# A transformer stack with a routed expert layer on one core: the router's placement compared in halves and summed inside a context layer, context layer 5 behind the expert tiles, and the third norm's second root ahead of the copies

## The chip, the cores and the metric

The kernel runs on one core of a Trainium2 chip. The metric is the device time of one execution in microseconds. The kernel before was executed three times for its time and once more under the profiler.

## What is computed

Eight blocks of 100 tokens with 256 features, `x`, pass through four residual steps, each behind a layer norm (mean and variance of a token, epsilon 1e-5). What matters of the reference:

```python
x = x + jnp.tanh(g_xattn[0]) * _L0_xattn_ref(_layernorm(x), ctx_768, ...)   # attention over 361 context rows
x = x + jnp.tanh(g_ffn[0]) * _L0_ffn_ref(_layernorm(x), w_router, w1, b1, w2, b2)
x = x + jnp.tanh(g_xattn[1]) * _L1_xattn_ref(_layernorm(x), ctx_768, ...)   # ternary weights, int8 activations
x = x + jnp.tanh(g_ffn[1]) * _L1_ffn_ref(_layernorm(x), ...)                # 16 heads chosen by a gate

# _L0_ffn_ref
sel = jnp.argmax(softmax(x @ w_router), axis=-1)      # one of 8 experts for each token
for e in range(8):
    y = relu(x @ w1[e] + b1[e]) @ w2[e] + b2[e]
    out = out + ((sel == e) * wgt)[:, None] * y

# _L1_xattn_ref, for each of two attention layers Wa, and a linear layer before
qx = clip(round(x / i_scale), -128, 127);  i_scale = max(abs(x)) / 127
kv = bitnet_linear(image_embeds, Wa, ba)
```

## The kernel before, in words

The program is written by hand: each engine has a list of instructions in program order, and semaphores (`S[...]`) are the only link between the lists. Nothing is scheduled by a tool. TensorE is PE, VectorE is DVE, ScalarE is ACT, GpSimd is POOL, and SyncE (SP) issues most loads. T is 800 tokens, a half is 400 tokens or blocks 0 to 3 and 4 to 7. The stages, in order of time: the first attention; its residual and the second norm; the router; the expert tiles; the third norm; the second attention; its feed-forward part; the fourth norm; the gated heads.

**The router's placement.** Tokens are sorted by expert into tiles of 128 slots. DVE finds, for each token, its tile (`at_tile`, L859 and L861) and its slot in the tile as a row of 128 zeros and ones (`at_slot`, one compare of 100x1024 elements at L863, which increments `placed`). PE sums `at_slot` times `at_tile` over the eight blocks into bank 3 (L1709, eight matmuls of 28 columns, two instructions each). DVE makes of it `token_of`, the token in each slot (L866, L868), and increments `inverse_done`. POOL then gathers the rows of the first tiles from `x_slots` in DRAM with indirect DMAs (L483).

**Context layers.** The keys and values of the second attention don't hang on `x`. PE computes them as filler, as `last_context_layer(b)` for eight blocks b: four matmuls for keys (L1499) and six for values (L1507), in the rotating banks 4 to 7. ACT evicts each layer with two ACTIVATEs (L1313) and three copies (L1318), and increments `kv_out` five times. Layer 0 stands behind the router's scores, layers 1 to 3 between the rank matmuls and the sum L1709, layers 4 and 5 behind that sum, and 6 and 7 behind the expert tiles.

**Expert tiles.** PE waits for the evictions of six layers (`kv_out` at 30), `inverse_done` and the first gather (`xs_in0`), turns that tile (L1720, in bank 6, one of the rotating ones) and enters the loop over 14 tiles: 16 matmuls of two instructions for the hidden part (L1736), the turn of the next tile, and 8 such for the result (L1749). DVE adds the bias (L894), POOL scatters to `y_slots` (L489). SP loads each expert's weights into two buffers, released by PE's counts.

**The third norm.** SP loads `y_slots` back in four pairs of blocks. DVE adds them to `x` (L908), takes statistics of each block (L533, one block behind), gathers them for each half (L551) and writes the variance (L557, `ln_var`). ACT takes the root (L1176, `ln_std`). DVE makes its reciprocal (L563) and the shift (L564, `ln_shift`). ACT normalises blocks 0 to 3, 6 and 7 (L1179), DVE blocks 4 and 5 (L568). PE turns each half in two steps (L1451), and ACT copies each step to `xT` (L1183). On ACT one function, `layernorm_by_halves`, does root, normalisation and two copies of half 0, and then the same of half 1. DVE then takes the maxima of `xT` (L932), and through POOL's reduction over partitions the scale; it quantises `xT` (L602, L603), and PE's matmuls of the text projection start (L1457). The second norm uses the same functions with k = 2.

Of the kernel before, what the change touches and what calls it, by code (L numbers as in the profile page):

```python
# [6 lines left out]
ALU = mybir.AluOpType  # L7
ACT = mybir.ActivationFunctionType
# [11 lines left out]
HT = T // 2  # L20
# [17 lines left out]
         [(1, j) for j in range(0, 6)], [(1, j) for j in range(6, 12)], [(1, j) for j in range(12, 16)]]  # L38
OWN = (0, 3, 6)
NP = 4  # L40
NW = 3
# [88 lines left out]
def flamingo(nc, d):  # L130

    ctx = ExitStack()
    with ctx:
# [389 lines left out]
        def _(dve):  # L523
# [35 lines left out]
            def half_shift(k, h):  # L559

                bs = slice(4 * h, 4 * h + 4)
                dve.wait_ge(S["ln_std"], 2 * (k - 1) + h)
                link(dve.reciprocal(rstd[:, bs], std[:, bs]))  # L563
                dve.scalar_tensor_tensor(var[:, bs], mv[:, bs, 0], -1.0, rstd[:, bs], ALU.mult, ALU.mult)\  # L564
                    .then_inc(S["ln_shift"], 1)
                if h == 1:
                    for b in (4, 5):
                        dve.tensor_scalar(xn[:, b, :], x[:, b, :], mv[:, b, 0:1], rstd[:, b:b + 1],  # L568
                                          ALU.subtract, ALU.mult).then_inc(S["ln_out"], 1)
# [256 lines left out]
            for z in range(3):  # L826
                ins = dve.tensor_tensor(lead[:, z + 1, 4:12, :], lead[:, z, 4:12, :],
                                        lead[:, z, 4 - 2 ** z:12 - 2 ** z, :], ALU.add)
                if z < 2:
# [32 lines left out]
                              const("token", N)[:, :, None].to_broadcast([N, B, TILES]), ALU.mult)  # L862
            dve.tensor_tensor(at_slot, along_b(const("slot", N), SLOTS),  # L863
                              r_s[:, :, None].to_broadcast([N, B, SLOTS]), ALU.is_equal).then_inc(S["placed"], 1)
            dve.wait_ge(S["inverse_mm"], 1)
# [39 lines left out]
            for b in range(B + 1):  # L905
                if b < B:
                    dve.wait_ge(S[f"gathered{b // 2}"], 16)
                    dve.scalar_tensor_tensor(x[:, b, :], y_tok[:, b, :], top_w[:, b:b + 1], x[:, b, :],  # L908
                                             ALU.mult, ALU.add).then_inc(S["x2_done"], 1)
                if b >= 1:  # L910
                    dve.wait_ge(S["x2_done"], b)
                    ins = token_stats(b - 1)
                if b == 4:
                    link(ins)
                    link(gather_stats(0, 4))
                    half_variance(0)
                if b == 5:
                    half_shift(3, 0)
                if b == 7:
                    link(ins)  # L920
                    gather_stats(4, 7)
# [236 lines left out]
        def _(act):  # L1158
# [11 lines left out]

            def layernorm_by_halves(k):

                for h in range(2):
                    bs = slice(4 * h, 4 * h + 4)
                    act.wait_ge(S["ln_var"], 2 * (k - 1) + h)
                    act.activation(std[:, bs], var[:, bs], ACT.Sqrt).then_inc(S["ln_std"], 1)  # L1176
                    act.wait_ge(S["ln_shift"], 2 * (k - 2) + h + 1)
                    for b in range(4) if h == 0 else (6, 7):
                        act.activation(xn[:, b, :], x[:, b, :], ACT.Identity, bias=var[:, b:b + 1],  # L1179
                                       scale=rstd[:, b:b + 1]).then_inc(S["ln_act"], 1)  # L1180
                    for kk in range(2):
                        act.wait_ge(S["ln_turned"], 4 * (k - 1) + 2 * h + kk + 1)
                        act.copy(xT[:, kk, h * HT:(h + 1) * HT], psum[4 + 2 * kk + h][:, 0:HT])\  # L1183
                            .then_inc(S["xT_ready"], 1)

# [108 lines left out]
            for n in range(8):  # L1294
# [3 lines left out]
                               bias=cols[:, 4 + m:5 + m]).then_inc(S["h0_out"], 1)  # L1298
            layernorm_by_halves(2)
            act.wait_ge(S["logit_a"], 1)  # L1300
# [19 lines left out]

            for b in range(6):
                last_context_out(b)
# [9 lines left out]

            last_context_out(6)
            last_context_out(7)
            layernorm_by_halves(3)
            act.wait_ge(S["quantised"], 4)
# [92 lines left out]
        def _(pe):  # L1429
# [12 lines left out]
            def turn_tokens_half(k, h):  # L1442

                for kk in range(2):
                    for g in range(4):
                        b = 4 * h + g
                        if b in (4, 5):
                            pe.wait_ge(S["ln_out"], B + 2 * (k - 2) + b - 3)
                        else:
                            pe.wait_ge(S["ln_act"], 6 * (k - 2) + (b if b < 4 else b - 2) + 1)  # L1450
                        ins = pe.transpose(psum[4 + 2 * kk + h][:, g * N:(g + 1) * N], xn[:, b, kk * P:(kk + 1) * P],  # L1451
                                           ident[0:N, 0:N])
                    ins.then_inc(S["ln_turned"], 1)
# [31 lines left out]
            for n in range(4):  # L1485
                m, half = n // 2, n % 2
                layer(psum[4 + n][:, 0:HT], lambda k: w_q[:, k, m * P:(m + 1) * P],
                      lambda k: xT[:, k, half * HT:(half + 1) * HT], 2, 2).then_inc(S["q_mm"], 1)
            def last_context_layer(b):

# [3 lines left out]
                for m in range(2):  # L1494
                    j = 5 * b + m
                    if j >= 4:
                        pe.wait_ge(S["kv_out"], j - 3)
                    for k in range(2):
                        ins = pe.matmul(psum[4 + j % 4][:, 0:M], wa[m][:, k, :], qc[:, k, b, :],  # L1499
                                        start=k == 0, stop=k == 1)  # L1500
                    ins.then_inc(S["kv_mm"], 1)
                for c, (c0, rows_c) in enumerate(CH):
                    j = 5 * b + 2 + c
                    if j >= 4:
                        pe.wait_ge(S["kv_out"], j - 3)
                    for k in range(2):
                        ins = pe.matmul(psum[4 + j % 4][0:rows_c, 0:D], qc[:, k, b, c0:c0 + rows_c],  # L1507
                                        wkv[:, k], start=k == 0, stop=k == 1)
                    ins.then_inc(S["kv_mm"], 1)

            def ternary(name, n):
# [192 lines left out]
            pe.matmul(psum[1][0:N, 0:B * E0], ones, before, start=False, stop=True).then_inc(S["rank_mm"], 1)  # L1704
            for b in range(1, 4):
                last_context_layer(b)
            pe.wait_ge(S["placed"], 1)
            for b in range(B):
                ins = pe.matmul(psum[3][0:SLOTS, 0:2 * TILES], at_slot[:, b, :],  # L1709
                                at_tile[:, b].rearrange("p z t -> p (z t)"), start=b == 0, stop=b == B - 1)  # L1710
            ins.then_inc(S["inverse_mm"], 1)
            last_context_layer(4)
            last_context_layer(5)
            pe.wait_ge(S["kv_out"], 5 * 6)
            pe.wait_ge(S["inverse_done"], 1)
# [38 lines left out]

            last_context_layer(6)
            last_context_layer(7)
            pe.wait_ge(S["kv_out"], 5 * B)
# [72 lines left out]
            def turn_half(h):  # L1830

                for kk in range(2):
                    for g in range(4):
                        b = 4 * h + g
                        pe.wait_ge(S["ln_out"], B + 4 + b + 1)
                        ins = pe.transpose(psum[(4 if h == 0 else 6) + kk][:, g * N:(g + 1) * N],
# [182 lines left out]
```

## Time and profile before

| | us |
|---|---|
| time, median of 3 executions | 660.27 |
| lowest and highest of them | 658.64 and 660.91 |
| the profiled execution's own time | 658.99 |
| its span, first to last instruction | 657.2 |
| PE busy | 596.5 (91%) |
| DVE busy | 327.0 (50%) |
| ACT busy | 217.8 (33%) |
| POOL busy | 71.0 (11%) |
| chain that ended last | PE 83%, DVE 8%, ACT 4%, DMA 2% |

The mean granted clock of PE was 0.938 of full speed. The span is what the profiler saw between the first and last instruction; the time holds what lies around it, here 1.8 us. An engine's busy time is a sum over stages of quite different limits. The chain of waits follows the work back from the last instruction, at each step to what released it. The timeline gives instructions in order of time, neighbours of one kind merged; its bracket says how long the engine was idle before and which work ended that.

### The profile page before, as it was taken

Reading aid. Unit: us, or ns where it says so; the run is one execution under the profiler, and the core shown is the slowest. Engines: PE = TensorE matmul, PEld = TensorE weight load, DVE = VectorE, ACT = ScalarE, POOL = GpSimd, SP = SyncE. Lnnn points to the kernel's source line nnn. Section 1 sums busy time; section 2 is a strip of 40 time slices with the busy share of each in tenths; the row PEclk is TensorE's granted clock in tenths of the full one; section 3 lists DMA queues with packets and bytes.
Section 4 is the critical chain, followed back from the end, with each engine's and each line's share of the span. In section 5 each row is a group of like instructions: output and inputs, shape, how many; then the busy total and the mean of one; then the engine's idle time right before and its main releaser. Section 6 shows DMA issues by size and latency. Waiting matters only on the chain.

```text
span 657.2 us, 9281 instructions
## 1 busy us (share of the span) xinstructions
PE 596.5 (91%) x3603; PEld 393.2 (60%) x3603; DVE 327.0 (50%) x772; ACT 217.8 (33%) x508; POOL 71.0 (11%) x69
## 2 busy tenths in 40 slices
PE   6989999999979899999995489776699999999997
PEld 4755344444555778999994267445365555555653
DVE  3686766588746551212223567689624223221543
ACT  2543665656633363122114454381110000000100
POOL 0052000000017002232221000000100100000000
PEclk9999999999989969999998589687699999999999
DMA  8900000000016235999982000600443553330000
GB/s 204 331 13 17 1 1 1 2 2 2 2 33 205 71 126 185 335 332 347 341 308 67 0 0 6 220 0 1 135 138 96 188 206 96 97 96 1 0 26 25
DMA packets 25194, 69.93 MB, mean 106 GB/s; under 512 B 5142, under 2 KB 12918, under 8 KB 21318
## 3 DMA queue, kind: packets, MB, share of 16 engines
q1 hardware_dynamic: 21798, 58.16, 26.9%
q0 software_dynamic: 3360, 11.28, 4.9%
q8 instruction: 24, 0.39, 0.2%
q14 instruction: 12, 0.10, 0.0%
HBM read 64.62 MB, written 4.80 MB: 106 GB/s over the span
## 4 chain that ended last, share of the span: by engine, by line
PE 83%; DVE 8%; ACT 4%; DMA 2%; issue 1%; POOL 1%; SPq 0%; DVEq 0%; ACTq 0%; POOLq 0%
PE bank L1869 20%; PE bank L1457 12%; PE bank L1736 8%; PE bank L1749 7%; PE bank L1588 7%; PE bank L1905 7%; PE bank L1562 5%; PE bank L1606 3%; PE bank L1797 2%; PE bank L1531 2%; PE bank L1779 2%; PE bank L1594 1%; ACT region L1362 1%; PE bank L1800 1%; PE bank L1787 1%
## 5 line engine op out<-in xcount | busy, mean ns | idle before, releaser
L1869 PE MATMUL bank<-region,kvT 128*128 128x400 f32 x384 | 132.4, 506 | 0.3 <-DVE region L1080 0.3
L1869 PEld LDWEIGHTS bank<-region,kvT 128*128 128x128 f32 x384 | 73.4, 193 | 56.5 <-issue 3.4
L1086 DVE TENSOR_TENSOR region<-xT,stage 128x800 f32<-128x800 f32 x30 | 29.7, 991 | 73.7 <-PE bank L1869 73.5
L690 DVE TENSOR_REDUCE nmax<-bank 100x2 f32<-100x722 f32 x64 | 55.2, 904 | 16.4 <-PE bank L1562 15.9
L1736 PEld LDWEIGHTS bank<-stage,region 128*128 128x128 f32 x448 | 52.1, 192 | 1.4 <-issue 0.8
L1736 PE MATMUL bank<-stage,region 128*128 128x128 f32 x448 | 52.4, 275 | 0.5 <-ACT stage L1306 0.5
L1749 PE MATMUL bank<-region,stage 128*128 128x256 f32 x224 | 50.7, 379 | 0.0
L1749 PEld LDWEIGHTS bank<-region,stage 128*128 128x128 f32 x224 | 41.5, 190 | 5.1
L1905 PE MATMUL bank<-region,kvt 128*128 128x400 f32 x128 | 43.9, 500 | 0.0
L1588 PE MATMUL bank<-xT,kvt 64*121 64x400 f32 (+1 forms) x144 | 38.9, 543 | 1.5 <-ACT kvT L1285 0.6
L888 DVE TENSOR_SCALAR stage<-bank,stage 128x128 f32<-128x128 f32 x56 | 15.8, 344 | 48.8 <-PE bank L1736 48.8
L1329 ACT ACTIVATE stage<-bank,stage 128x128 f32<-128x128 f32 x56 | 16.0, 368 | 66.6 <-PE bank L1736 31.7
L1905 PEld LDWEIGHTS bank<-region,kvt 128*128 128x128 f32 x128 | 24.0, 190 | 17.5
L1112 DVE TENSOR_TENSOR region<-region,stage 128x400 f32<-128x400 f32 x32 | 18.2, 574 | 31.4 <-PE bank L1905 31.3
L1457 PE MATMUL bank<-region,w_a 96*128 96x361 f32 x64 | 23.8, 519 | 7.0 <-DMA cols<-in_cols 6.3
L1285 ACT ACTIVATE region<-bank 121x400 f32<-121x400 f32 (+1 forms) x48 | 21.6, 501 | 23.0 <-PE bank L1594 23.0
L1285 ACT ACTIVATE kvT<-bank 121x400 f32<-121x400 f32 (+1 forms) x48 | 21.8, 501 | 19.8 <-PE bank L1594 19.7
L1562 PE MATMUL bank<-kvt,xT 32*100 32x361 f32 x192 | 24.6, 502 | 2.3 <-POOL xT L456 1.2
L894 DVE TENSOR_TENSOR stage<-bank,stage 128x256 f32<-128x256 f32 x14 | 5.9, 424 | 35.3 <-PE bank L1749 35.3
L1457 PE MATMUL bank<-w_a,region 96*121 96x256 f32 (+1 forms) x96 | 22.4, 384 | 0.0
L1457 PEld LDWEIGHTS bank<-region,w_a 96*128 96x128 f32 x64 | 12.7, 207 | 15.7 <-DMA cols<-in_cols 6.3
L1588 PEld LDWEIGHTS bank<-xT,kvt 64*121 64x121 f32 (+1 forms) x144 | 13.3, 178 | 14.5 <-ACT kvT L1285 4.3
(328 smaller groups left out, 903.6 us busy)
## 6 DMA issues: line engine op xcount, KB each, us to landing
region<-in_e_w SPq DMA_DIRECT2D x28, 1024.0 KB, 5.1
kvT<-in_p_qkv SPq DMA_DIRECT2D x32, 384.0 KB, 3.1
stage<-w_dram POOLq DMA_DIRECT2D x2, 1600.0 KB, 12.2
stage<-in_t_f SPq DMA_DIRECT2D x1, 2048.0 KB, 14.8
kvt<-in_p_o SPq DMA_DIRECT2D x1, 2048.0 KB, 9.5
stage<-in_e_b SPq DMA_DIRECT2D x14, 128.0 KB, 6.5
region<-in_ctxT SPq DMA_DIRECT2D x3, 541.5 KB, 14.5
stage<-w_dram POOLq DMA_DIRECT2D x1, 1200.0 KB, 9.1
```

What stands on the lines that cost most here:

```text
L690: dve.tensor_reduce(nmax[:, b % 2, at_h:at_h + 9:8], banks[0:N, bank:bank + 2, 0:M], AX.X, ALU.max, negate=True)\
L1086: dve.tensor_tensor(x_w[n % NW], xT[:, :, at_h], w_bc[h][:, None, e, :].to_broadcast([P, 2, HT]), ALU.mult).then_inc(S["xw_done"], 1)
L1112: dve.tensor_tensor(z_w[n % NW], oT[h], w_bc[h][:, e, :], ALU.mult).then_inc(S["z_done"], 1)
L1285: act.activation(probsT[n % 2][0:rows_c, c, g].rearrange("p j n -> p (j n)"), psum[4 + y % 3][0:rows_c, 0:4 * N], ACT.Exp).then_inc(S["y_o ...
L1457: ins = pe.matmul(bank, w(k), src(k), start=start and k == 0, stop=stop and k == kk - 1)
L1562: ins = pe.matmul(psum[i + (4 if b == 0 else 0)][0:N, 0:M], qm[b % 3][at_i, t, 2 * (i % 2) + par, :], kT[at_i, t, b, :], start=True, stop= ...
L1588: pe.matmul(bank[g], kT[at_g, t, b, c0:c0 + rows_c], qm[b % 3][at_g, t].rearrange("p j n -> p (j n)"), start=True, stop=False)
L1606: ins = pe.matmul(psum[7][32 * i:32 * i + VW, w * N:(w + 1) * N], v_b[b][0:rows_c, c, 8 * t + 2 * i + par, :], probsT[b % 2][0:rows_c, c, ...
L1736: ins = pe.matmul(psum[2 * u + m // 4][:, (m % 4) * P:(m % 4 + 1) * P], e_w1[u][:, k, m * P:(m + 1) * P], xsT[u][:, k, :], start=k == 0, s ...
L1749: ins = pe.matmul(psum[4 + u][:, 0:D], hsT[u][:, m, :], e_w2[u][:, m, :], start=m == 0, stop=m == KF - 1)
L1869: ins = pe.matmul(psum[3 * h + j][:, 0:HT], p_w[n % NP][:, k, j * HE:(j + 1) * HE], x_w[n % NW][:, k, :], start=e == 0 and k == 0, stop=e ...
L1905: ins = pe.matmul(psum[3 * h + m][:, 0:HT], o_all[:, e, m * P:(m + 1) * P], z_w[n % NW], start=e == 0, stop=e == E1 - 1)
```

## The change

The edits, one by one:

- On DVE `at_slot` is compared in two halves of four blocks, each with its own increment of `placed`. PE waits for the first ahead of block 0 of the sum and for the second ahead of block 4.
- On PE `last_context_layer` is cut into `last_context_keys` and `last_context_values`. The sum stands between the keys and the values of layer 3.
- Layer 5 moves from ahead of the expert tiles to behind them, on PE and on ACT. The wait ahead of the tiles is for 25 evictions, not 30.
- In the third norm, DVE makes reciprocal and shift of half 0 ahead of the statistics of block 4, and normalises blocks 4, 5 and 6 (`SHARE[3]` is 7; for the second norm it stays at 6). ACT normalises block 7 alone in half 1.
- On ACT `layernorm_by_halves` is cut into three functions. The second norm calls them in the old order; the third takes the root of half 1 ahead of the copies of half 0.
- The counts waited for by later turns follow.

```diff
+SHARE = {2: 6, 3: 7}
...
                 if h == 1:
-                    for b in (4, 5):
+                    for b in range(4, SHARE[k]):
                         dve.tensor_scalar(xn[:, b, :], x[:, b, :], mv[:, b, 0:1], rstd[:, b:b + 1],
...
-            dve.tensor_tensor(at_slot, along_b(const("slot", N), SLOTS),
-                              r_s[:, :, None].to_broadcast([N, B, SLOTS]), ALU.is_equal).then_inc(S["placed"], 1)
+            for h in range(2):
+                bs = slice(4 * h, 4 * h + 4)
+                dve.tensor_tensor(at_slot[:, bs], const("slot", N)[:, None, :].to_broadcast([N, 4, SLOTS]),
+                                  r_s[:, bs, None].to_broadcast([N, 4, SLOTS]), ALU.is_equal).then_inc(S["placed"], 1)
...
+                if b == 5:
+                    half_shift(3, 0)
                 if b >= 1:
                     dve.wait_ge(S["x2_done"], b)
                     ins = token_stats(b - 1)
...
-                if b == 5:
-                    half_shift(3, 0)
...
-            for b in range(6):
+            for b in range(5):
                 last_context_out(b)
             turn_tile(0, 1)
...
-            last_context_out(6)
-            last_context_out(7)
-            layernorm_by_halves(3)
+            for b in range(5, B):
+                last_context_out(b)
+            half_root(3, 0)
+            half_normalise(3, 0)
+            half_root(3, 1)
+            half_turned(3, 0)
+            half_normalise(3, 1)
+            half_turned(3, 1)
...
-            for b in range(1, 4):
-                last_context_layer(b)
-            pe.wait_ge(S["placed"], 1)
+            last_context_layer(1)
+            last_context_layer(2)
+            last_context_keys(3)
             for b in range(B):
+                if b % 4 == 0:
+                    pe.wait_ge(S["placed"], b // 4 + 1)
                 ins = pe.matmul(psum[3][0:SLOTS, 0:2 * TILES], at_slot[:, b, :],
                                 at_tile[:, b].rearrange("p z t -> p (z t)"), start=b == 0, stop=b == B - 1)
             ins.then_inc(S["inverse_mm"], 1)
+            last_context_values(3)
             last_context_layer(4)
-            last_context_layer(5)
-            pe.wait_ge(S["kv_out"], 5 * 6)
+            pe.wait_ge(S["kv_out"], 5 * 5)
             pe.wait_ge(S["inverse_done"], 1)
...
-            last_context_layer(6)
-            last_context_layer(7)
+            for b in range(5, B):
+                last_context_layer(b)
```

How the order changes on PE between layer 3 and the first tile's turn. Before (L1499 keys, L1507 values, L1709 the sum, L1720 the turn):

```order
L1499 MATMUL bank<-stage,tern 128x361 x4
L1507 MATMUL bank<-tern,stage 121x256 x4
L1507 MATMUL bank<-tern,stage 119x256 x2
L1709 MATMUL bank<-stage 128x28 x8
L1499 MATMUL bank<-stage,tern 128x361 x4
L1507 MATMUL bank<-tern,stage 121x256 x4
L1507 MATMUL bank<-tern,stage 119x256 x2
L1499 MATMUL bank<-stage,tern 128x361 x4
L1507 MATMUL bank<-tern,stage 121x256 x4
L1507 MATMUL bank<-tern,stage 119x256 x2
L1720 MATMUL bank<-consts,stage 128x128 x2
```

In the changed kernel the same place reads (L1516 keys, L1527 values, L1736 the sum, L1747 the turn):

```order
L1516 MATMUL bank<-stage,tern 128x361 x4
L1736 MATMUL bank<-stage 128x28 x8
L1527 MATMUL bank<-tern,stage 121x256 x4
L1527 MATMUL bank<-tern,stage 119x256 x2
L1516 MATMUL bank<-stage,tern 128x361 x4
L1527 MATMUL bank<-tern,stage 121x256 x4
L1527 MATMUL bank<-tern,stage 119x256 x2
L1747 MATMUL bank<-consts,stage 128x128 x2
```

The sum has moved ahead of the six value matmuls of layer 3, and the ten matmuls of layer 5 are gone from here.

On ACT, the third norm before (L1176 root, L1179 normalisation, L1183 copies):

```order
L1176 ACT_TABLE_LOAD
L1176 ACTIVATE std<-var 100x4
L1179 ACTIVATE xn<-x,var,rstd 100x256 x4
L1183 COPY xT<-bank 128x400 x2
L1176 ACTIVATE std<-var 100x4
L1179 ACTIVATE xn<-x,var,rstd 100x256 x2
L1183 COPY xT<-bank 128x400 x2
```

and in the changed kernel (L1178, L1184, L1191):

```order
L1178 ACT_TABLE_LOAD
L1178 ACTIVATE std<-var 100x4
L1184 ACTIVATE xn<-x,var,rstd 100x256 x4
L1178 ACTIVATE std<-var 100x4
L1191 COPY xT<-bank 128x400 x2
L1184 ACTIVATE xn<-x,var,rstd 100x256
L1191 COPY xT<-bank 128x400 x2
```

The second root stands ahead of the first two copies, and one of the two normalisations of half 1 is gone from ACT.

## Rows read from the trace of the kernel before

**Rows 1.** The page's chain that ended last, by engine.
```profile
PE 83%; DVE 8%; ACT 4%; DMA 2%; issue 1%; POOL 1%; SPq 0%; DVEq 0%; ACTq 0%; POOLq 0%
```

**Rows 2.** The chain of waits, router to first tile: start us, us, what.
```profile
229.43 2.84 PE bank L1457 x16
...
241.57 0.86 PE bank L1507 x6
242.43 1.71 PE bank L1709 x16
```

**Rows 3.** Timeline of the same stretch: start us, us, engine, line, operation [idle before].
```profile
239.67 0.27 DVE L859 TENSOR_TENSOR stage<-r_c,consts 100x112 f32<-100x112 f32 x1
...
240.18 1.22 DVE L863 TENSOR_TENSOR stage<-consts,r_s 100x1024 f32<-100x1024 f32 x1
...
244.38 0.17 DVE L868 TENSOR_TENSOR token_of<-bank,spare 128x14 uint32<-128x14 f32 x1
...
245.43 1.10 POOL L483 DMA_INDIRECT stage<-x_slots,token_of  x1 [36.67 <-DVE token_of L868]
...
245.57 0.92 ACT L1318 COPY kvt<-bank 121x256 f32<-121x256 f32 x3
...
247.44 0.96 ACT L1318 COPY kvt<-bank 121x256 f32<-121x256 f32 x3
...
248.46 0.43 PE L1720 MATMUL bank<-consts,stage 128*128 128x128 f32 x2 [0.93 <-ACT kvt L1318]
```

**Rows 4.** The line of the gathers, L483, all 15 of them.
```profile
DMA to landing us min/median/max: 2.7/5.5/5.8
```

**Rows 5.** Windows: busy us of each engine, then PE's granted clock, DMA share, GB/s.
```profile
226.00:228.00 2.00, 1.03 (x5) 0.68 (x6) 1.09 (x5) 1.25 (x3) 0.00 (x0) 0.78 0.97 266
...
240.50:241.00 0.50, 0.50 (x5) 0.38 (x4) 0.50 (x1) 0.48 (x3) 0.00 (x0) 0.72 0.00 0
...
248.00:248.50 0.50, 0.04 (x1) 0.05 (x1) 0.00 (x0) 0.40 (x2) 0.00 (x0) 1.00 0.00 0
...
356.00:357.00 1.00, 0.00 (x0) 0.00 (x0) 0.00 (x0) 0.98 (x2) 0.00 (x0) 0.92 0.64 226
...
472.00:473.00 1.00, 1.00 (x3) 0.39 (x2) 0.90 (x6) 0.00 (x0) 0.00 (x0) 0.55 0.93 342
```

**Rows 6.** The page's groups: busy us, mean ns | idle before, what ended it.
```profile
L1736 PE MATMUL bank<-stage,region 128*128 128x128 f32 x448 | 52.4, 275 | 0.5 <-ACT stage L1306 0.5
```

**Rows 7.** The chain of waits through the third norm.
```profile
351.86 2.43 DMA y_slots<-stage,token_of
...
361.87 0.34 DVE stats L533
...
369.09 0.50 ACT xT L1183
...
373.84 1.69 PE bank L1457 x6
```

**Rows 8.** Timeline of layer 7's eviction and the third norm.
```profile
356.09 1.28 ACT L1176 ACT_TABLE_LOAD   x1
...
364.84 0.17 DVE L557 TENSOR_SCALAR var<-mv 100x4 f32<-100x4 f32 x1
...
365.77 0.49 ACT L1183 COPY xT<-bank 128x400 f32<-128x400 f32 x1 [0.17 <-PE bank L1451]
366.16 0.21 ACT L1176 ACTIVATE std<-var 100x4 f32<-100x4 f32 x1
...
366.70 0.73 DVE L568 TENSOR_SCALAR xn<-x,mv,rstd 100x256 f32<-100x256 f32 x2
366.81 1.09 ACT L1179 ACTIVATE xn<-x,var,rstd 100x256 f32<-100x256 f32 x2 [0.44 <-DVE var L564]
...
367.44 1.04 DVE L932 TENSOR_REDUCE umax<-xT 128x1 f32<-128x400 f32 x2
```

**Rows 9.** Timeline of PE at the start of the gated heads.
```profile
468.86 6.60 PE L1869 MATMUL bank<-region,kvT 128*128 128x400 f32 x13 [0.32 <-DVE region L1080]
```

More of the change, by code:

```diff
@@ L1169, in layernorm_turn, with half_root, half_normalise, half_turned @@
                     act.copy(xT[:, kk, half * HT:(half + 1) * HT], psum[4 + n][:, 0:HT]).then_inc(S["xT_ready"], 1)
[L1171 to L1184, printed above, removed]
+            def half_root(k, h):
+                bs = slice(4 * h, 4 * h + 4)
+                act.wait_ge(S["ln_var"], 2 * (k - 1) + h)
+                act.activation(std[:, bs], var[:, bs], ACT.Sqrt).then_inc(S["ln_std"], 1)
+            def half_normalise(k, h):
+                act.wait_ge(S["ln_shift"], 2 * (k - 2) + h + 1)
+                for b in range(4) if h == 0 else range(SHARE[k], B):
+                    act.activation(xn[:, b, :], x[:, b, :], ACT.Identity, bias=var[:, b:b + 1],
+                                   scale=rstd[:, b:b + 1]).then_inc(S["ln_act"], 1)
+            def half_turned(k, h):
+                for kk in range(2):
+                    act.wait_ge(S["ln_turned"], 4 * (k - 1) + 2 * h + kk + 1)
+                    act.copy(xT[:, kk, h * HT:(h + 1) * HT], psum[4 + 2 * kk + h][:, 0:HT]).then_inc(S["xT_ready"], 1)
             def context_out(b):
@@ L1298, in _ @@
                                bias=cols[:, 4 + m:5 + m]).then_inc(S["h0_out"], 1)
-            layernorm_by_halves(2)
+            for h in range(2):
+                half_root(2, h)
+                half_normalise(2, h)
+                half_turned(2, h)
             act.wait_ge(S["logit_a"], 1)
@@ L1446, in turn_tokens_half @@
                         b = 4 * h + g
-                        if b in (4, 5):
+                        if 4 <= b < SHARE[k]:
                             pe.wait_ge(S["ln_out"], B + 2 * (k - 2) + b - 3)
+                        elif b >= 4:
+                            pe.wait_ge(S["ln_act"], 6 * (k - 2) + 4 + b - SHARE[k] + 1)
                         else:
-                            pe.wait_ge(S["ln_act"], 6 * (k - 2) + (b if b < 4 else b - 2) + 1)
+                            pe.wait_ge(S["ln_act"], 6 * (k - 2) + b + 1)
                         ins = pe.transpose(psum[4 + 2 * kk + h][:, g * N:(g + 1) * N], xn[:, b, kk * P:(kk + 1) * P],
@@ L1488, in _, with last_context_keys @@
                       lambda k: xT[:, k, half * HT:(half + 1) * HT], 2, 2).then_inc(S["q_mm"], 1)
-            def last_context_layer(b):
+            def last_context_keys(b):
                 if b == 0:
@@ L1501, in last_context_layer, with last_context_values @@
                     ins.then_inc(S["kv_mm"], 1)
+            def last_context_values(b):
                 for c, (c0, rows_c) in enumerate(CH):
@@ L1509, in last_context_layer @@
                     ins.then_inc(S["kv_mm"], 1)
+            def last_context_layer(b):
+                last_context_keys(b)
+                last_context_values(b)
             def ternary(name, n):
@@ L1834, in turn_half @@
                         b = 4 * h + g
-                        pe.wait_ge(S["ln_out"], B + 4 + b + 1)
+                        pe.wait_ge(S["ln_out"], B + 5 + b + 1)
                         ins = pe.transpose(psum[(4 if h == 0 else 6) + kk][:, g * N:(g + 1) * N],
```

## The prediction

> **What bounds the kernel now.** I read the chain of waits first, then the timeline at the two places where it leaves TensorE (PE), then the granted clock. PE holds 83% of the chain that ended last [rows 1]: a change that takes away no matmul can only win where PE stands still or where the chain leaves it. Two such places lie beside the lines of the diff.
>
> The first is the way into the expert tiles. The chain runs through context layer 3, the sum of the placement (L1709) and layers 4 and 5 [rows 2], whose last links are evictions by ScalarE (ACT), to the turn of the first gathered tile, L1720 [rows 3]. Behind it PE works without a break: L1736's matmuls had 0.5 us of idle time ahead of them, all of it before the first [rows 6]. So the loop starts when L1720 may start, and all later work moves with it.
>
> The second is the third norm. After the last expert result the chain goes at 351.86 us into a scatter, a load, VectorE (DVE) and ACT, and is back for good with the matmuls at 373.84 [rows 7]. PE does layers 6 and 7 in that gap, then waits. What counts here is the round of DVE, ACT, PE, ACT and DVE.
>
> **The placement, compared in halves and summed earlier.** The compare L863 (100x1024) starts at 240.18 and takes 1.22 us, so it ends at 241.40 [rows 3]. PE comes to the sum only at 242.43, after the value matmuls of layer 3, 0.86 us from 241.57 [rows 2]. PE is late, not DVE. Now the sum stands ahead of those six matmuls and can begin at 241.57, 0.86 us earlier. The split makes two compares of 512 elements. From L863 (1024 elements, 1.22 us) and L859 (112 elements, 0.27 us) [rows 3] an element costs (1.22 - 0.27) / 912 = 1.04 ns and the fixed part is 0.15 us; the halves take 0.69 us each and end at 240.87 and 241.56. The first four blocks need one of them at 241.57, the last four the other some 0.86 us later. So the split by itself is worth nothing here, since one compare would be done at 241.40, and its 0.15 us on DVE are hidden by DVE's wait for the sum. It would pay if PE came 0.2 us sooner.
>
> The sum ends 0.86 us earlier, and with it token_of (244.38) and the first gather, issued by GpSimd (POOL) at 245.43 [rows 3]. The quickest gathers landed 2.7 us after their issue [rows 4]: 248.13 before, 247.27 now. POOL has nothing else queued. SP's reloads in the loop wait for PE's own counts and move with it.
>
> **Context layer 5, moved behind the tiles.** L1720 starts at 248.46, right behind ACT's copies of layer 5 (247.44 and 0.96 us) [rows 3]; the gather was there at 248.13. Layer 5 thus costs 0.33 us beyond it. Now PE waits for five layers. Layer 4 starts where it did (241.57 + 1.71 + 0.86 = 244.14 in either order), so its last copy still ends at 245.57 + 0.92 = 246.49 [rows 3]. The gather decides, at 247.27 and 0.03 us of waking: L1720 moves from 248.46 to 247.30, **1.16 us**. Bounds: 0.33, if the gather is issued no earlier (between token_of's end at 244.55 and the issue lie 0.88 us [rows 3] that no row explains, and something that does not move may sit in them); 1.97, if it lands before ACT is done. I take 1.16, since release and landing both have rows. Behind the tiles the layer costs ACT what lies between two neighbouring layers, 247.44 - 245.57 = 1.87 us [rows 3]: the last copy ends at 357.95 for 356.08, the table load of 1.28 us behind it at 359.23 [rows 8]. The first root is wanted 0.3 us ahead of the rstd, to which the chain comes at 361.87 + 0.34 = 362.21 [rows 7] and now 0.34 us sooner, so by 361.5. That leaves 2.3 us of cover, and the layer costs nothing; if the loads of y_slots were 2.3 us faster the cover would be gone.
>
> **The first half's shift ahead of block 4's statistics.** These hold 0.34 us of the chain, at 361.87 [rows 7]. What follows in the first half, ACT's four normalisations, PE's turns and their release of ACT's copies, comes 0.34 us earlier. DVE does the same work in all, so the second half's var stays at 364.84 + 0.17 = 365.01 [rows 8].
>
> **The root ahead of the copies.** ACT took the second root at 366.16, behind the copy begun at 365.77 [rows 8], though var was ready at 365.01. Now it starts at 365.04, **1.12 us** earlier. The copies wait for its 0.21 us: 365.25 to 365.74 and on to 366.23, where they ended at 365.77 + 0.49 = 366.26 before. The 0.34 us of the step above pay for the root; without them the copies would be some 0.2 us late.
>
> **The shares.** DVE's xn of blocks 4 and 5 start 1.13 us earlier, at 365.57 for 366.70; a third adds 0.37 and ends at 366.67. ACT's single one starts behind the copies, at 366.23, takes 0.55 and ends at 366.78; the second of its two ended at 366.81 + 1.09 = 367.90 [rows 8]. Had ACT kept two, it would be 367.32: 0.54 of the gain hangs on SHARE. PE's last turns and ACT's last copy (369.09 [rows 7]) move by 1.12 us, to 367.97. DVE's first two maxima (1.04 us [rows 8]), begun some 0.2 us behind the third xn, end at 367.9, before the last copy does, so they don't hold the last maximum. From there to the matmuls at 373.84 all is serial. Gain: **1.12 us**. Bounds: 0.58, if the third tile on DVE is of no use; 1.46, if the 0.34 us came on top.
>
> **Sum.** -1.16 - 1.12 = -2.28 us. The profiled execution took 658.99 us for its span of 657.2, and would take 656.7. It is the second fastest of four (658.64 to 660.91). From the median of 660.27 the same step leads to 658.0, which is my number. A measurement of this kernel tells about 0.3%, 2.0 us, from no change; the gain lies at that edge.
>
> **The clock, which can take the gain back.** PE's granted clock rose to its full 2.4 GHz at about 240.8, and it held through the gap around L1720, where PE had been idle for 0.93 us [rows 3, 5]. After layers 6 and 7 and then no work at all it fell to half, 1.2 GHz, within 356 to 357 [rows 5]. The change makes the stretch ahead of L1720 look more like that one: it had layers 4 and 5 in it and then 0.93 us of waiting, now it has layer 4 alone, done 1.87 us sooner, and about 1.6 us of waiting. The row at 248 speaks for the sum as it stands, -2.28 us. The Trainium skill, "TensorE: Matmul & The Clock Gate", section "Part 1: The HAM clock gate (the "warmup" mystery)", says that the half clock is the default and that only activity releases it; by that the loop may start at half clock and the sum is rival B's. Of that rule the trace shows both sides: agreement at 356, and at 248 a gap too short to matter.
>
> **Rivals.**
> A, as summed: 658.0. Chance 0.45.
> B, the clock falls around L1720 in most executions, and the loop's first matmuls run at 1.2 GHz until it rises. Nearest rows: the dense matmuls that began at 468.86 had the half clock until 472.9 [rows 5, 9], 4.0 us, of which half is lost, 2.0 us. That gives 660.0, and less where it rises sooner. For it: the thinner work. Against: it held in the trace. The skill's page on the clock gate stands behind this one. 0.27.
> C, the gather comes no earlier, as bounded: 660.27 - 0.33 - 1.12 = 658.8. For it: the unexplained 0.88 us. 0.14.
> D, slower: the clock falls at the same place and stays down as it did from 227.1 to 240.8 [rows 5], 13.7 us, though PE worked from 229.43 on, first on the router's scores [rows 2]. Half of it, 6.8 us, on 658.0 makes 664.8. It decides from 4.6 us at half clock on, where the loss passes 2.3, and is beyond 0.3% from 8.5 us on. Against: those scores write 8 columns a matmul, the loop's matmuls 128 and 256. 0.07.
> E, the change doesn't do what it says: another wait takes each place (a bank of layer 3 not yet evicted, a late third xn), and the two gains together stay under half a microsecond. 659.9. 0.07.
>
> **How the numbers follow.** The range goes from 656.7, which the bounds of 1.97 and 1.46 from the median (656.8) and the sum from the profiled execution both give, to 660.3, which takes in B, C and E. D and the far tails are left out. Faster by over 0.3% means under 658.3: A gives it in two of three cases (0.31), B and C now and then (0.07): 0.38. Slower by over 0.3%: D, and a little of B and E: 0.09. The rest, 0.53, is no difference that can be told.
>
> **What would show it.** The sum's matmuls right behind four key matmuls, with the first gather 0.9 us nearer to them; L1720's counterpart waiting for a DMA, not for ACT; full clock in the first 4 us of the loop; ACT's second root within 0.1 us of DVE's var; and from the last tile's scatter to the text matmuls 20.9 us where it was 22.0 (351.86 to 373.84 [rows 7]). I am wrong if the turn still follows an eviction, if the loop's first matmuls run at half clock, or if that distance is unchanged.

## The result and the profile after

The changed kernel is slower: 661.34 us median (659.13 to 663.48, 20 executions), against 659.40 (657.53 to 661.18, 20) for the kernel before, whose three executions shown ahead had been on the high side. The ratio is 1.0032, with a 95% interval of 1.0020 to 1.0043: 2.1 us lost where 2.3 were to be won.

| | before | after |
|---|---|---|
| time, median of 20, us | 659.40 | 661.34 |
| the profiled execution's own time, us | 658.99 | 663.48 |
| its span, us | 657.2 | 661.6 |
| PE's mean granted clock in it | 0.938 | 0.928 |
| PE busy, us | 596.5 | 602.5 |

The profiled execution of the changed kernel is the slowest of its 20. Stage by stage, between the starts of instructions that both traces have (worked out from the two timelines):

| from | to | before | after | difference |
|---|---|---|---|---|
| the first instruction | the router's first scores | 224.35 | 225.99 | +1.64 |
| these | the sum of the placement | 17.92 | 16.91 | -1.01 |
| the sum | the first tile's turn | 6.19 | 6.12 | -0.07 |
| the turn | the loop's first matmul | 0.97 | 1.20 | +0.23 |
| that | the load of y_slots | 104.93 | 108.61 | +3.68 |
| the load | the text matmuls | 19.48 | 18.38 | -1.10 |
| these | the first scores of the second attention | 5.54 | 5.57 | +0.03 |
| these | its feed-forward part | 42.62 | 43.44 | +0.82 |
| that | the gated heads' first matmul | 46.86 | 47.13 | +0.27 |

The first line has nothing to do with the edits: no instruction differs there. In the trace after, the granted clock was at half between 64.6 and 71.5 us, in the one before it was not. The two traces are so 4.5 us apart where the medians are 1.9 apart. The two gains of the sum are there (-1.01 and -1.10), and most of the loss sits in the loop; the +0.82 ahead of the feed-forward part comes with a clock at half until 388.9, through the first scores, where before it was at half until 377.3 and from 380.7 to 384.1. The changed kernel's timeline of PE, DVE and POOL around its start, with the answers to [rows 2, 3]:

```profile
242.90 1.87 PE L1736 MATMUL bank<-stage 100*128 100x28 f32 x16
...
245.01 0.17 DVE L871 TENSOR_TENSOR token_of<-bank,spare 128x14 uint32<-128x14 f32 x1
...
246.06 1.10 POOL L484 DMA_INDIRECT stage<-x_slots,token_of  x1 [35.39 <-DVE token_of L871]
...
249.02 0.66 PE L1747 MATMUL bank<-consts,stage 128*128 128x128 f32 x2 [2.01 <-DMA stage<-x_slots,token_of]
...
250.22 6.47 PE L1763 MATMUL bank<-stage,region 128*128 128x128 f32 x32 [0.54 <-ACT stage L1316]
```

The turn no longer waits for ACT but for the gather, as summed: 3.0 us behind the issue (246.06 to 249.02, where 2.7 were reckoned). PE stood still for 2.01 us ahead of it. The last row is the first tile's hidden part: 32 matmul instructions in 6.47 us. In the trace before the same row reads 3.83 us. The windows say why (columns as in [rows 5]):

```profile
248.00:249.00 1.00, 0.00 (x0) 0.01 (x1) 0.00 (x0) 0.00 (x0) 0.43 (x1) 0.98 0.31 102
249.00:250.00 1.00, 0.66 (x2) 0.28 (x2) 0.00 (x0) 0.29 (x1) 0.05 (x1) 0.50 0.46 131
...
254.00:255.00 1.00, 1.00 (x6) 1.00 (x6) 0.00 (x0) 0.89 (x4) 0.00 (x0) 0.50 0.00 0
255.00:256.00 1.00, 1.00 (x8) 1.00 (x7) 0.00 (x0) 0.25 (x1) 0.00 (x0) 0.61 0.00 0
256.00:257.00 1.00, 1.00 (x11) 0.97 (x10) 0.21 (x1) 0.05 (x1) 0.00 (x0) 1.00 0.00 0
```

The granted clock fell to half at 248.96, ahead of the turn, and rose at 255.8, so the loop's first 5.56 us, from 250.22 on, ran at 1.2 GHz; half of that is 2.8 us. From the loop's first matmul to the start of the last tile's L897 (before L894) it is 104.71 us for 101.73. The page shows it in the group that answers to [rows 6], 55.0 us for 52.4:

```profile
L1763 PE MATMUL bank<-stage,region 128*128 128x128 f32 x448 | 55.0, 284 | 0.5 <-ACT stage L1316 0.5
```

A further 0.7 us of the loop's line is the last scatter, which took 3.14 us to land where it had taken 2.43. The chain of waits through the third norm, beside [rows 7]:

```profile
355.63 3.14 DMA y_slots<-stage,token_of
...
369.52 0.21 ACT std L1178
...
372.45 0.50 ACT xT L1191
...
377.21 1.69 PE bank L1474 x6
```

and its timeline, beside [rows 8]:

```profile
361.76 1.28 ACT L1178 ACT_TABLE_LOAD   x1
...
369.31 0.17 DVE L558 TENSOR_SCALAR var<-mv 100x4 f32<-100x4 f32 x1
...
369.52 0.21 ACT L1178 ACTIVATE std<-var 100x4 f32<-100x4 f32 x1 [0.78 <-DVE var L558]
369.63 0.87 ACT L1191 COPY xT<-bank 128x400 f32<-128x400 f32 x2
...
370.05 1.05 DVE L569 TENSOR_SCALAR xn<-x,mv,rstd 100x256 f32<-100x256 f32 x3
370.39 0.61 ACT L1184 ACTIVATE xn<-x,var,rstd 100x256 f32<-100x256 f32 x1
```

The second root follows its variance by 0.04 us (it was 1.15 late), and stands on the chain itself. The table load ends at 363.04, 2.95 us ahead of the first root at 365.99.

### The profile page after: what moved, and what is told of

Same layout as the page of the kernel before. It is cut to its first block, busy times and chain, and to the rows that moved or that the text cites. A ratio compares the mean times of both kernels' runs of the same rounds, so it can differ in the third digit from the quotient of the medians.

```text
span 661.6 us, 9282 instructions
## 1 busy us (share of the span) xinstructions
PE 602.5 (91%) x3603; PEld 396.6 (60%) x3603; DVE 327.5 (50%) x774; ACT 216.7 (33%) x507; POOL 71.1 (11%) x69
## 4 chain that ended last, share of the span: by engine, by line
PE 82%; DVE 8%; ACT 3%; DMA 3%; issue 2%; POOL 1%; SPq 0%; ACTq 0%; DVEq 0%; POOLq 0%
PE bank L1896 20%; PE bank L1474 10%; PE bank L1763 8%; PE bank L1776 7%; PE bank L1613 7%; PE bank L1932 7%; PE bank L1587 5%; PE bank L1631 3%; PE bank L1806 2%; PE bank L1556 2%; PE bank L1824 2%; DMA region<-in_ctxT 2%; PE bank L1619 2%; ACT region L1377 1%; PE bank L1827 1%
## 5 line engine op out<-in xcount | busy, mean ns | idle before, releaser
L1763 PEld LDWEIGHTS bank<-stage,region 128*128 128x128 f32 x448 | 54.8, 200 | 1.6 <-issue 0.9
L1763 PE MATMUL bank<-stage,region 128*128 128x128 f32 x448 | 55.0, 284 | 0.5 <-ACT stage L1316 0.5
L1613 PE MATMUL bank<-xT,kvt 64*121 64x400 f32 (+1 forms) x144 | 40.4, 566 | 1.5 <-ACT kvT L1292 0.6
L897 DVE TENSOR_TENSOR stage<-bank,stage 128x256 f32<-128x256 f32 x14 | 5.9, 425 | 35.4 <-PE bank L1776 35.4
L1613 PEld LDWEIGHTS bank<-xT,kvt 64*121 64x121 f32 (+1 forms) x144 | 13.7, 185 | 15.1 <-ACT kvT L1292 4.3
L490 POOL DMA_INDIRECT y_slots<-stage,token_of x14 | 13.9, 995 | 76.6 <-DVE stage L897 76.6
```

The source lines that it names most:

```text
L1613: pe.matmul(bank[g], kT[at_g, t, b, c0:c0 + rows_c], qm[b % 3][at_g, t].rearrange("p j n -> p (j n)"), start=True, stop=False)
L1763: ins = pe.matmul(psum[2 * u + m // 4][:, (m % 4) * P:(m % 4 + 1) * P], e_w1[u][:, k, m * P:(m + 1) * P], xsT[u][:, k, :], start=k == 0, s ...
```

## The experiments

Three theories after the result. **Theory 1:** with layer 5 gone PE does too little ahead of the first turn, the clock falls, and the loop's start runs at half of it. **Theory 2:** the new place of the sum, or something else in the two edits ahead of the loop, causes it. A third question came up on the way: whether the norm's microsecond arrives at the end of the kernel. Every kernel but `one_compare_share6`, which was only profiled, was timed with the kernel before beside it on the same chip: 12 executions where nothing else is said, against 23 to 35 of the kernel before. Four kernels shared each chip. A ratio is an estimate of its own with its 95% interval; the quotient of the two medians can differ from it by 0.0015.

**One edit at a time.** `layer_only` is the kernel before with

```diff
             last_context_layer(4)
-            last_context_layer(5)
-            pe.wait_ge(S["kv_out"], 5 * 6)
+            pe.wait_ge(S["kv_out"], 5 * 5)
...
-            last_context_layer(6)
-            last_context_layer(7)
+            for b in range(5, B):
+                last_context_layer(b)
```

and the same on ACT.

> The kernel before with one edit: context layer 5 behind the expert tiles on PE and ACT (wait for 25 evictions), the sum of the placement where it was, one compare, third norm as before. Theory 1 (the clock): with layer 5 gone PE stands still for over 1.5 us ahead of the first tile's turn, its granted clock falls to half there and the loop's first 6 to 7 us run at it; the time is 1 to 3 us ABOVE before, about 661. Theory 2 (the loss belongs to the new place of the sum, not to the layer): the clock holds, the turn comes 0.3 us earlier, the time is within 0.5 us of before.

Measured: 661.38 us against 659.14, ratio 1.0037 (1.0022 to 1.0052). Its waits of PE, and its windows:

```profile
PE bank L1741 <- DMA stage<-x_slots,token_of: 2.8, 1, 2.8
```

```profile
248.00:249.00 1.00, 0.00 (x0) 0.00 (x0) 0.00 (x0) 0.00 (x0) 0.85 (x1) 0.90 0.41 106
...
251.00:254.00 3.00, 3.00 (x14) 3.00 (x15) 0.00 (x0) 0.00 (x0) 0.63 (x1) 0.50 0.15 44
254.00:256.00 2.00, 2.00 (x13) 2.00 (x12) 0.00 (x0) 1.14 (x4) 0.00 (x0) 0.60 0.00 0
```

The wait for the gather is 2.8 us, in it the clock falls (0.90 in the window from 248), and it is back at 255.6. From the loop's first matmul to the load of y_slots it is 107.82 us, 2.89 more than in the kernel before. This one edit costs all that the whole change costs.

`sum_only` has the two compares and the sum ahead of layer 3's values, and layer 5 where it was:

```diff
-            for b in range(1, 4):
-                last_context_layer(b)
+            last_context_layer(1)
+            last_context_layer(2)
+            last_context_keys(3)
...
             ins.then_inc(S["inverse_mm"], 1)
+            last_context_values(3)
             last_context_layer(4)
             last_context_layer(5)
```

> The kernel before with one edit: compare in two halves and the sum ahead of layer 3's value matmuls; layer 5 stays ahead of the tiles, third norm as before. Theory 1 (the clock falls for want of layer 5): clock full around the first tile's turn, the turn still waits for ACT's copies of layer 5, so the earlier gather is worth nothing: time within 0.5 us of before. Theory 2 (the sum's new place lets the clock fall): the loop's first 6 us at half clock, 2 to 3 us above before.

Measured: 659.04 against 659.14, ratio 1.0004 (0.9981 to 1.0026). The turn still waits for ACT's copies, 7.04 us behind the sum's start for 6.19, and the clock was full from 239.8 to 359.2:

```profile
249.56 0.44 PE L1746 MATMUL bank<-consts,stage 128*128 128x128 f32 x2 [0.92 <-ACT kvt L1328]
```

The expectation had the turn waiting there, and nothing lost. Theory 2 is out for the sum's place. `norm_only` has the third norm's edits alone:

```diff
+SHARE = {2: 6, 3: 7}
...
-            layernorm_by_halves(3)
+            half_root(3, 0)
+            half_normalise(3, 0)
+            half_root(3, 1)
+            half_turned(3, 0)
+            half_normalise(3, 1)
+            half_turned(3, 1)
```

with DVE's shift of half 0 ahead of block 4's statistics.

> The kernel before with the third norm's edits alone (shift of half 0 ahead of block 4's statistics, second root ahead of the copies, blocks 4 to 6 on DVE). Both theories: 1.1 us below before, about 658.3, and from the load of y_slots to the text matmuls 18.4 us for 19.5. If instead part of the loss sits here (the clock stays low longer behind the norm), the time is no lower than before.

Measured: 658.72 against 659.14, ratio 0.9991 (0.9975 to 1.0007). From the load of y_slots to the text matmuls it is 18.56 us for 19.48, so the norm gains 0.92 us where it is; the time can't confirm it. More on this below.

**Giving PE something to do.** `fill12` is the changed kernel with twelve throw-away matmuls, ahead of PE's wait for the first tile:

```diff
             last_context_layer(4)
+            for r in range(12):
+                pe.matmul(psum[0][:, 0:M], wa[0][:, r % 2, :], qc[:, r % 2, 4, :], start=True, stop=True)
             pe.wait_ge(S["kv_out"], 5 * 5)
```

> The changed kernel with twelve key matmuls of layer 4 done once more into bank 0, which nobody reads, between layer 4 and the wait for the first tile (about 1.9 us of PE at full clock, in a gap of 2.0 us). Theory 1 (the clock): it holds over the turn, the loop runs at full clock, and both gains come through: 1.5 to 2.3 us below before, about 657.5. Theory 2 (the loss has another cause than PE standing still there): the time stays at the changed kernel's, 661, or above it.

Measured: 657.15 against 659.14, ratio 0.9979 (0.9962 to 0.9995), where the changed kernel had 1.0032: 3.5 us less by the two ratios, with more work in it. Timeline and window:

```profile
248.77 2.00 PE L1742 MATMUL bank<-stage,tern 128*128 128x361 bf16 x12
251.00 0.41 PE L1749 MATMUL bank<-consts,stage 128*128 128x128 f32 x2 [0.23 <-DMA stage<-x_slots,token_of]
```

```profile
251.00:253.00 2.00, 1.46 (x11) 1.23 (x12) 0.00 (x0) 0.37 (x1) 0.94 (x1) 1.00 0.22 66
```

The turn starts 6.18 us behind the sum, as in the changed kernel (6.12), so the fillers delay nothing; the clock is full, and loop to load takes 104.94 us, as before the change. This settles theory 1: the same edits, the same waits, only PE busy. The profiled execution was the slowest of its 12 (661.90); 3.2 us of that lie ahead of the router's first scores (at 227.53 for 224.35), where no instruction differs. So the trace speaks for the loop here and the median for the time. Over all fourteen traces of this document, loop to load takes 104.9 to 105.2 us in the twelve whose clock was full there, and 107.8 and 108.6 in the two whose clock was at half. The mean granted clock of an execution agrees: its median is 0.933 in the changed kernel's 20 and 0.935 in `layer_only`, against 0.938 in the kernel before (35 executions beside these runs) and in `fill12`.

`fill6` does the same with six.

> The changed kernel with six repeated key matmuls, half as many, so that PE still stands still for about 1.1 us ahead of the turn, a little more than in the kernel before (0.93). Theory 1: what decides is how much PE does ahead of the turn, so this lies between: either the clock holds, 657.2, or it falls in part of the executions, and the times spread between 657 and 661 with a median near 658.5. Theory 2 (only an unbroken stretch of work holds it): the changed kernel's 661.

Measured: 657.37 against 659.74, ratio 0.9971 (0.9952 to 0.9991). In its trace PE still stood still for 1.15 us ahead of the turn, and the clock held. Six do as well as twelve, as far as 12 executions of each on two chips can tell.

`layer_fill` is `layer_only` with the twelve.

> The kernel before with layer 5 behind the tiles and twelve repeated key matmuls of layer 4 ahead of the wait for the first tile; sum and norm as before. With layer 5 alone moved it was 1.0037 of before. Theory (the clock): the loop runs at full clock, the turn waits for the gather as in that run, 0.3 us ahead of before: 0.999 to 1.000. Rival (the three layers behind the tiles cost something there): still 1.5 us or more above before.

Measured: 658.96 against 659.15, ratio 0.9997 (0.9981 to 1.0013). The loss of `layer_only` is gone, so none of it came from the layers behind the tiles; and what the layer's move alone gives is too small to tell from nothing here.

`front_fill` is `fill12` with the third norm as before.

> The changed kernel with its twelve repeated key matmuls ahead of the first tile, but with the third norm as before (old order on ACT and DVE, blocks 6 and 7 on ACT). Theory 1 (the two gains are independent and the clock alone took them back): the turn comes about 1 us earlier than in the kernel before and the loop runs at full clock, so about 1.0 us below before, 658.1. Rival (the third norm's edits carry all the gain of the filled kernel): no lower than before.

Measured: 659.34 against 659.74, ratio 0.9990 (0.9973 to 1.0008), on another chip than `fill12`. The expected 1.0 us lies inside the interval, and so does no gain at all.

**Compare and shares.** `one_compare_share6` is `fill12` with one compare and `SHARE = {2: 6, 3: 6}`.

> The filled kernel (twelve matmuls) with one compare of 1024 elements and with blocks 6 and 7 of the third norm on ACT again, the order of root and copies as changed. By the working of the prediction: the sum starts no later behind layer 3's keys (the compare ends some 0.2 us before PE comes), and the last of the two normalisations ends 0.54 us later than the one, so that the way from ACT's second root to the last copy of xT is 0.5 us longer.

Measured: 657.91 us, a single execution. Timeline of PE at the sum:

```profile
242.88 1.97 PE L1733 MATMUL bank<-stage 100*128 100x28 f32 x16 [0.58 <-DVE stage L864]
```

PE waited 0.58 us for the compare. The clock had risen at 239.8, 10.2 us after its fall, for 13.7 us in the trace before; layer 2 and the keys of layer 3 ran at full clock, and PE came earlier than DVE. The expectation missed this. The trace of `sum_only` has two halves and the same rise, at 239.8: there the sum started 16.51 us behind the router's first scores, here 16.95, so the split is worth 0.44 us in such an execution. The way from ACT's second root to the last copy's start is 3.15 us (365.82 to 368.97), against 2.93 in the changed kernel: the third tile on DVE is worth 0.22 us, not 0.54, since PE's eight turns at half clock, 1.91 us with the new shares, are themselves the longest piece.

**The other gap.** `warm` is `fill12` with fourteen more, behind the norm's turns:

```diff
             turn_tokens_half(3, 1)
+            for r in range(14):
+                pe.matmul(psum[0][:, 0:HT], wa[0][:, r % 2, :], tern[:, a0:a0 + HT], start=True, stop=True)
             pe.wait_ge(S["simsq_done"], 1)
```

> The filled kernel (twelve matmuls) with fourteen more throw-away matmuls of 400 columns behind the third norm's turns, ahead of the wait for the quantised tokens, where PE stands still for 4.8 us at half clock. If idle PE is what keeps the clock down there too, the text matmuls (1.7 us at half clock) and the first scores run at full clock: 1 to 2.5 us below the filled kernel, about 655.5. Rival: the chain there is DVE's and ACT's, and the matmuls behind it gain less than 0.5 us.

Measured: 656.12 against 659.74, ratio 0.9934 (0.9912 to 0.9956; 6 executions). It beats both kernels:

```profile
368.39 4.52 PE L1792 MATMUL bank<-tern 128*128 128x400 bf16 x14
...
373.39 0.59 PE L1474 MATMUL bank<-simsq,consts 128*128 128x16 f32 x4 [0.48 <-DVE stage L604]
```

```profile
372.00:374.00 2.00, 1.51 (x10) 0.83 (x9) 1.21 (x2) 0.00 (x0) 0.00 (x0) 0.90 0.00 0
```

The clock is up at 372.4, and from the text matmuls to the first scores it is 4.61 us for 5.57. It was at half again from 379.2 to 382.6, so the first scores, which began at 378.0 and took 2.70 us, still ran at half for more than half of their time; they were expected at full. `full_one_compare` is `warm` with one compare again.

> The changed kernel with both groups of throw-away matmuls (twelve and fourteen) and one compare of 1024 elements in place of two halves. With two halves it was 0.9934 of before. By the prediction the split is worth nothing: 0.993 again. By the run with one compare and the old shares, where the clock rose 3.4 us earlier against the work and PE waited 0.58 us for the compare, it is worth up to 0.6 us in such executions: 0.9935 to 0.9945.

Measured: 655.62 against 659.15, ratio 0.9961 (0.9942 to 0.9980; 11 executions). The lowest median of all. By the ratio it gained less than either expectation had: 0.993 lies under its interval, and of 0.9935 to 0.9945 only the upper end lies in it. The interval overlaps that of `warm`, and by the quotient of medians the two are equal (0.9946 and 0.9945). What the split is worth on average stays open. In its trace the clock rose at 240.5 and the sum followed the keys without a wait.

**Where the norm's microsecond goes.** `before_warm` and `norm_warm` have the fourteen matmuls, the first with the old norm, the second with the new.

> The kernel before with fourteen throw-away matmuls of 400 columns behind the third norm's turns, nothing else. The filled kernel with them came to 0.9934 of before, without them to 0.9979. Theory (the scores of the second attention run at half clock because PE stands still under the norm's chain): about 2 to 3 us below before, 657. Rival (what they gained hung on the third norm's edits): within 1 us of before.

> The kernel before with the third norm's edits and the same fourteen matmuls. Theory (alone, the norm's 1 us was lost again because the clock rose no sooner, so that more of the scores ran at half clock): with the clock up early the norm's whole 1.0 us shows, 1.0 us below the run with these matmuls and the old norm. Rival (the norm's edits cost something behind the norm): no difference between the two.

Measured: 657.47 and 657.32 against 659.15, ratios 0.9970 (0.9953 to 0.9987) and 0.9973 (0.9953 to 0.9993). The fourteen matmuls alone gain 2 us; the norm's edits on top show nothing. In their traces load to text is 18.54 for 19.39, a gain of 0.85, but from the first scores to the feed-forward part it is 41.77 for 40.70: with the new norm the clock was at half from 376.5 to 379.9, over the first scores, with the old one it was full. The traces of the kernel before and of `norm_only` show what can happen, since their clocks fell at the same instants (227.1 and 227.2, 356.8 and 356.9). Kernel before, then `norm_only`:

```profile
376.00:378.00 2.00, 1.48 (x5) 0.43 (x3) 0.00 (x0) 2.00 (x4) 0.00 (x0) 0.67 0.00 0
378.00:380.00 2.00, 0.62 (x2) 0.42 (x3) 1.07 (x2) 1.49 (x2) 0.00 (x0) 1.00 0.00 0
380.00:382.00 2.00, 1.96 (x5) 0.54 (x3) 1.54 (x4) 1.20 (x4) 0.00 (x0) 0.68 0.00 0
```

```profile
376.00:378.00 2.00, 0.60 (x2) 0.00 (x0) 0.64 (x1) 1.98 (x3) 0.00 (x0) 0.50 0.00 0
378.00:380.00 2.00, 1.51 (x3) 0.91 (x4) 0.43 (x2) 0.62 (x1) 0.00 (x0) 0.50 0.00 0
380.00:382.00 2.00, 2.00 (x4) 0.66 (x3) 1.27 (x4) 0.85 (x3) 0.00 (x0) 0.50 0.00 0
```

Text matmuls came at 372.93 for 373.84. But with the old norm the clock was up from 377.3 to 380.7 and the first scores (L1779) took 2.59 us; with the new one it stayed down until 384.2 and they (L1803) took 3.90. The value matmuls then start at the same time:

```profile
385.81 0.83 PE L1797 MATMUL bank<-stage,kvt 121*128 121x100 f32 x6
```

```profile
385.94 0.83 PE L1821 MATMUL bank<-stage,kvt 121*128 121x100 f32 x6
```

In this pair the whole 0.91 us was given back in 7 us, and not for good: the next fall of the clock came at 414.9 in the kernel before and only at 418.3 in `norm_only`, and the last value matmuls lay between the two.

```profile
414.82 1.59 PE L1797 MATMUL bank<-stage,kvt 121*128 121x100 f32 x6
```

```profile
414.94 0.91 PE L1821 MATMUL bank<-stage,kvt 121*128 121x100 f32 x6
```

The feed-forward part began at 421.17 for 422.00, the gated heads at 468.47 for 468.86. So what the norm's edits are worth hangs on where the clock's changes fall. From the load of y_slots to the feed-forward part it is 65.48 and 65.73 us in `layer_fill` and `front_fill`, with the old norm, and 65.63 and 65.85 in `fill6` and `fill12`, with the new one: nothing gained there either. In four of the six traces with the old norm the first scores ran wholly at full clock, in none of the eight with the new one; whether that is more than chance is open. How much is lost on average is not settled: the comparisons have intervals wider than the effect.

## Why the prediction was wrong, point by point

- **Placement and gather: right.** Sum 1.01 us earlier against the scores (0.86 forecast), gather 0.88 us behind token_of's end as before, so that gap moves with it, and rival C is out. Of the 1.01, some 0.15 is luck: the clock rose 16.14 us behind the scores, for 16.43 before, and PE gains half of the 0.29. In `fill12` it rose 16.93 behind them, and the sum gained 0.62. From the end of layer 3's keys to the turn it is 5.96 us for 6.89: a gain of 0.93 for 1.16, as PE moved 3.0 us behind the gather's issue, not 2.7.
- **"The split by itself is worth nothing here": wrong in general.** It holds in the trace it was read from, and the prediction named the condition under which it fails, PE 0.2 us sooner. In an execution whose clock rose 3.4 us sooner after its fall, PE waited 0.58 us for one compare, and the split was worth 0.44.
- **Layer 5 behind the tiles "costs nothing": wrong, and this is the step that failed.** Its cost behind the tiles is nothing, as worked out, with 2.95 us of cover left. What I left out of the sum, which counted the move as part of a gain of 1.16 us, was what the layer did where it stood: it kept PE at work. Without it the loop started at half clock, and that cost 2.98 us. The section on the clock named this, weighed one row in which the clock held against one in which it fell, and took the first; the second was the likelier. The gap grew from 0.93 to 2.01 us, not to 1.6. Rival B, given 0.27, is what happened, though with a longer stretch at half clock than its 4.0 us: 5.56, past the 4.6 from which the prediction itself had reckoned with a slower kernel.
- **B's price was too small.** 2.0 us forecast, from the heads' first matmuls; measured 2.98 us on the loop in the trace after, as the clock stayed down for 5.56 us of it. In `layer_only` the loop starts 0.73 us later at nearly the same fall and rise (248.8 and 255.6) and less of it lies at half clock (4.7 us): an earlier turn is half eaten there. This, with the norm's gain lost again further on, would explain why the whole change (1.0032), with two gains more, stands hardly below `layer_only` (1.0037); no run isolates it.
- **The third norm: right in its place, wrong at the end.** Load to text 1.10 us shorter (1.12 forecast), 0.85 to 0.92 in two pairs that differ in it alone. "From there to the matmuls all is serial" was true, but I took the gain for good behind them, and PE's matmuls behind them ran at half clock there. The 0.54 us that were to hang on SHARE measured 0.22.
- **Level.** The 660.27 I started from was the median of three; of 20 it is 659.40. Against that my own sum would have read 657.1, and the filled kernel measured 657.15. That agreement is in part luck: its ratio of 0.9979 stands for 1.4 us, with an interval from 0.3 to 2.5, and the norm's half of the sum shows in no time.

## What to carry to other kernels

Filler work on TensorE has two uses, and a list of waits shows only one. Before moving it out of a gap, look at the granted clock in the next stretch: when the gap then leads straight into dense matmuls, a microsecond won at the wait can cost three behind it, as here (0.93 won, 2.98 lost). Throw-away matmuls into an unused bank, sized to end before the awaited data lands, are a cheap test of this, and here a cheap cure; it is also worth asking where else PE enters dense work at half clock.

## What the runs showed of the hardware that was not expected

- The clock fell in a wait of 2.0 us (`after`) and of 2.8 us (`layer_only`), each behind one context layer in bf16, and stayed at half for 6.8 us though PE was busy without a break for the last 5.6 and 4.7 of them. It held over 0.93 us behind two such layers and over 1.15 and 1.12 us behind one layer and six or twelve more matmuls (`fill6`, `layer_fill`).
- In the pair above, work that arrived 0.91 us earlier at a clock of half did not bring the full clock back any sooner, and at the value matmuls all of the 0.91 us was lost; 0.83 of it was there again at the feed-forward part, since the next fall missed the last matmuls ahead of it. The Trainium skill, "TensorE: Matmul & The Clock Gate", section "Part 1: The HAM clock gate (the "warmup" mystery)", says that the window in which the gate looks at activity runs free of the kernel. The pair agrees: the clock rose at 384.1 and 384.2 and at 425.1 and 425.2 in the two traces, while the work at the text matmuls was 0.91 us apart.
- Executions of one kernel differ by where these stretches fall. A stretch at half clock that begins between 64 and 67 us, in code that the change doesn't touch, stands in nine of the fourteen traces, `after` and `layer_only` among them, and not in those of the kernel before and `norm_only`. A single profile's end can so be 1.6 us off before the changed code is reached, and only distances between nearby instructions can be compared.
- The last scatter took 3.14 and 2.88 us in the two traces whose loop began at half clock, and 2.42 to 2.44 in the twelve others, the kernel before among them. Nothing here explains it.
